# Expert results of batch 0 written from the result slots into the merge's SBUF buffer, and the second attention's preparation placed four result products earlier

## The chip, the cores and the metric

The kernel runs on one core of one Trainium2 chip. The metric is the device time of the whole program in microseconds, the median of several runs.

## The reference

Eight batches of 512 tokens with 512 features go through two layers, each a gated cross-attention and a gated feed-forward:

```python
x = x + tanh(g_xattn[0]) * L0_xattn(layernorm(x), ctx, ctx, ...)
x = x + tanh(g_ffn[0])   * L0_ffn(layernorm(x), Wc, bc, W1, b1, W2, b2)
x = x + tanh(g_xattn[1]) * L1_xattn(layernorm(x), ctx, ctx, mask, ...)
x = x + tanh(g_ffn[1])   * L1_ffn(layernorm(x), W_r, W_k, W_v, mu_r, mu_k)
```

The part at issue is `L0_ffn`, a mixture of 128 experts over groups of 32 tokens (16 groups in a batch, 128 in all). In each group each expert takes the token with its largest logit, and puts its result back on that token:

```python
perm            = (logits == max over the group's tokens)
permuted        = einsum('bntd,bntes->bnesd', grouped, perm)
inner           = relu(einsum('bnesd,esdf->bnesf', permuted, W1) + b1)
result_permuted = einsum('bnesf,esdf->bnesd', inner, W2) + b2
result          = einsum('bnesd,bntes->bntd', result_permuted, perm)
```

## The kernel before

All loops over engines are written out by hand: `build` runs five parts one behind the other on each engine (keys and values; first attention; `experts`; second attention, which is `attention` with `merge` set; `feed_forward`), and semaphores are the only order between engines. All DMAs are issued by the sync engine (SP), in program order, so that a wait on it holds back everything behind it.

**Experts.** `gather` (L2101) picks the chosen tokens with products against the choices; ACT (L2012) and DVE (L2020) bring them from PSUM into `gt`, whose last axis is the group. A set `s` has 16 groups, one batch: four tiles of 128 tokens with four groups each. `hidden` (L2119) multiplies by W1. Then come 64 result products p (L2135). Each takes the 64 groups of four batches (`h = p // 32`), and makes four experts for the two PSUM banks: partition `c * 64 + group`, 512 features. ACT (L2031) and DVE (L2056) copy the banks into a ring of RO = 4 slots that lies over `chosen` and `xc1`; a slot is one block u (p = 2u and 2u + 1), 128 partitions x 4 experts x 512, 1 MB. SP stores each slot with one DMA (L1984) to DRAM (`s_rp`), and ACT and DVE wait, before they write block u, for the store of block u - 4 (`out_st`). Blocks 0 to 15 hold batches 0 to 3, blocks 16 to 31 batches 4 to 7.

**Merge.** The second attention begins behind the products. Its steps are called at fixed numbers p from `behind` in each engine and from `load_behind` on SP. At `MERGE_AT` = 41 PE adds the experts' results to the tokens of batch 0 (`merge_tile`, L1621 and L1622 for the bias b2, L1626 for the results in `rp`: 128 experts on partitions, 4 tiles x 4 groups x 512). DVE adds that to x and normalises (L1324, L1269, L1314). At `NORM_AT` = 45 PE transposes, at `QUERIES_AT` four query products follow, at `MAXIMA_AT` the maxima of the scores, at `ROWS_AT` = 58 the transpose of the maxima, and behind the last product (p = 63) the first scores (L1606). `result_on_act` gives ACT both copies of a product while DVE is at the merge.

**Loads for it.** Behind the store of block 16 (`HALF_U`), SP waits until blocks 0 to 15 have landed (`half_written`), and loads batch 0's results with 16 DMAs (`load_experts`, L709, one for each tile and group of four, 256 KB each, 128 rows of 2 KB); the query weight (L715) follows. Behind block 22 it loads batch 1's in the same way, when PE is through with `rp`. Batches from 1 on are loaded for each turn; from batch 2 on GpSimd adds the bias (L1050).

Of the kernel before, what the change touches and what calls it, by code (L numbers as in the profile page):

```python
# [79 lines left out]
MAXIMA_AFTER = {n: (k // 2, (0, 1) if k % 2 == 0 else (2, 3)) for k, n in enumerate((49, 50, 51, 52, 53, 54, 56, 57))}  # L80
MERGE_AT, WEIGHT_AT, NORM_AT, QUERIES_AT, ROWS_AT = 41, 43, 45, (47, 49, 51, 53), 58
MAXIMA_AT = {49 + n: (n // 2, (0, 1) if n % 2 == 0 else (2, 3)) for n in range(8)}
Ahead = namedtuple("Ahead", "load_weights load_first load_keys load_second load_output_weight constants first_norm query_weights_high query_weights_low first_norm_high "
# [3 lines left out]

Behind = namedtuple("Behind", "load act dve pe")

# [464 lines left out]
def attention(nc, lay, io, early, late, sem, eight, after, front=None, turned_place=None):  # L554
# [58 lines left out]
    if route:  # L613
        allot(early, "wqh wql kl mpick kbd vals pick bc mx xr wch wcl bcol tie nstats nmv nmark nve nn mt " + small)
        allot(late, "qh ql xth xtl woh wol ath pvs atl rs rx lg gmax perm chosen pr xn x")
        allot(turned_place, "mr")
    else:
        allot(early, "wqh wql xth xtl rp xn permb b2h b2l bo x qh ql pvs woh wol pr ath atl kbd kl mpick vals pick bc b2s mx "
                     "mt rs rx sums bq " + small)
# [85 lines left out]
    def load_experts(sp, j, t):  # L705
        of = 0 if isinstance(j, int) and j < HALF else 1
        src = io["rp"][of].rearrange("u (c j a t) s d -> (u c) s j t a d", c=2, a=GT, t=NT)
        for a in range(GT):
            sp.dma_start(rp[:, t, a:a + 1], src[:, :, bass.ds(j - HALF * of, 1), t, a]).then_inc(rp_in[t], 16)  # L709
# [167 lines left out]
    def load_behind(sp, u):  # L877


        if u is None:  # L880
            sp.wait_ge(front.cleared, 1)
            load_x(sp, 0)
        if u == 7:
            load_perm(sp, 0)
            sp.dma_start(b2[:, :], io["b2"]).then_inc(w_in[2], 16)
            load_gates(sp)
            sp.dma_start(bq[:, :], io["bq"]).then_inc(c_in, 16)
        if u == HALF_U:
            front.half_written(sp)
            for t in range(NT):  # L890
                load_experts(sp, 0, t)
            load_query_weight(sp)
        if u == HALF_U + 2:
            sp.wait_ge(const, 2)
            load_keys(sp, 0)
            sp.dma_start(bo[:, :], io["bo"].partition_broadcast(P)).then_inc(bo_in, 16)
        if u == 22:
            for k, uses in TW:
                sp.wait_ge(full[k], uses.n(None, "merge", 1) + 1)
            load_perm(sp, 1)  # L900
            for t in range(NT):
                load_experts(sp, 1, t)
        if u == 24:
            load_x(sp, 1)
        if u == 28:
            load_v(sp, 0)
# [118 lines left out]
    def gpsimd(pool):  # L1025
# [17 lines left out]
        def add_experts_bias(j, ts):  # L1043

            if isinstance(j, int) and j == 2 and 0 in ts:
                pool.wait_ge(b2_in, 16)
            for t in ts:
                pool.wait_ge(rp_in[t], 16 * GT * (j + 1))
                for a in range(GT):
                    pool.tensor_tensor(rp[:, t, a], rp[:, t, a], b2s[:, :], ALU.add).then_inc(rp_biased, 1)  # L1050
# [476 lines left out]
    def tensor(pe, banks_read=None, step_of=None):  # L1527
# [82 lines left out]
        def merge_tile(i, j, t):  # L1610
# [9 lines left out]
            else:  # L1620
                pe.matmul(out[:, :], permb[:, cols], b2h[:, :], start=True, stop=False, skip_group_check=True)  # L1621
                pe.matmul(out[:, :], permb[:, cols], b2l[:, :], start=False, stop=False, skip_group_check=True)  # L1622
                pe.wait_ge(rp_in[t], 16 * GT * (j + 1))
            for a in range(GT):
# [214 lines left out]
    if merge:  # L1839
        return Engines(sync, gpsimd, scalar, vector, tensor), banks_free, ident, mhalf, \  # L1840
            Behind(load_behind, lambda act, k: scalar(act, k), lambda dve, k: vector(dve, k),
                   lambda pe, k: tensor(pe, None, k))
    ahead = Ahead(load_weights, load_first, load_first_keys, load_second, load_output_weight, constants, first_norm, query_weights_high, query_weights_low,
# [5 lines left out]
def experts(nc, sb, sem, eight, io, behind):  # L1849
# [111 lines left out]
    def sync(sp):  # L1961
# [17 lines left out]
        for u in range(EK):  # L1979
            for p in (2 * u, 2 * u + 1):  # L1980
                for q in range(2):
                    b, n = result_bank(p, q)
                    sp.wait_ge(g_free[b], n + 1)
            sp.dma_start(io["rp"][2 * u // EK][u % (EK // 2)], slot(u)).then_inc(out_st[u % RO], 16)  # L1984
            behind[0].load(sp, u)

    def half_written(sp):
        for q in range(RO):
            sp.wait_ge(out_st[q], 16 * (EK // 2 // RO))

    def written(eng, q):
        eng.wait_ge(out_st[q], 16 * (EK // RO))

    def gathered(c, s, a):

        b, _ = use(SETS * c + s, a)
        ts = slice(TS * a, TS * (a + 1))
        dst = gt[:, :, s, :, ts] if turned(c) else gt[:, s, :, :, ts]
# [23 lines left out]
    def scalar(act):  # L2022
        def results(p):
            u = p // 2
            if p % 2 == 0 and u >= RO:
                act.wait_ge(out_st[u % RO], 16 * (u // RO))
            for q in range(2):
# [19 lines left out]
    def vector(dve):  # L2047
        def results(p):
            u = p // 2
            if p % 2 == 0 and u >= RO:  # L2050
                dve.wait_ge(out_st[u % RO], 16 * (u // RO))
            for q in range(2):
# [599 lines left out]
```

## Time and profile before

| | |
|---|---|
| median of 3 runs | 1321.31 us (1316.73 to 1325.94) |
| profiled execution | 1322.05 us, span 1320.3 us |
| PE busy | 1252.8 us (95% of the span) |
| DVE, ACT, POOL busy | 887.4, 570.1, 552.6 us |
| mean granted clock of PE | 0.986 of full speed |
| DMA | 213.59 MB, mean 162 GB/s |
| chain that ended last | PE 76%, DVE 9%, DMA 5%, sync queue 3%, issue 3%, ACT 3% |

The span is that of one profiled execution. "SPq" is SP's queue of DMA issues; the duration of an issue is the time that the queue spends on it, and its landing comes later. Names like `s_rp<-e_chosen` say where a transfer goes and where it comes from; the slots appear as `e_chosen` and `e_xc`. PE is matmul, ACT is ScalarE, DVE is VectorE, POOL is GpSimd. The granted clock is a share of full speed, 2.4 GHz; a half is the lower level, 1.2 GHz.

### The profile page before, as it was taken

Reading aid. Unit: us, or ns where it says so; the run is one execution under the profiler, and the core shown is the slowest. Engines: PE = TensorE matmul, PEld = TensorE weight load, DVE = VectorE, ACT = ScalarE, POOL = GpSimd, SP = SyncE. Lnnn points to the kernel's source line nnn. Section 1 sums busy time; section 2 is a strip of 40 time slices with the busy share of each in tenths; the row PEclk is TensorE's granted clock in tenths of the full one; section 3 lists DMA queues with packets and bytes.
Section 4 is the critical chain, followed back from the end, with each engine's and each line's share of the span. In section 5 each row is a group of like instructions: output and inputs, shape, how many; then the busy total and the mean of one; then the engine's idle time right before and its main releaser. Section 6 shows DMA issues by size and latency. Waiting matters only on the chain.

```text
span 1320.3 us, 28354 instructions
## 1 busy us (share of the span) xinstructions
PE 1252.8 (95%) x10607; PEld 901.3 (68%) x10607; DVE 887.4 (67%) x1570; ACT 570.1 (43%) x1039; POOL 552.6 (42%) x456
## 2 busy tenths in 40 slices
PE   8999999999999978886999999999998999999998
PEld 7777677777777657621447666766775778887887
DVE  6985677777676455564547766766685977777762
ACT  4255245534442554453562443353336434333331
POOL 3303642553251100000339657866834644454540
PEclk9999999999999998998999999999998999999999
DMA  9885465234411678899993643563423111111100
GB/s 351 220 184 185 138 183 173 79 113 150 142 65 45 209 206 273 308 402 368 403 337 116 213 167 99 176 221 123 133 84 129 64 64 64 64 49 47 64 29 35
DMA packets 126502, 213.59 MB, mean 162 GB/s; under 512 B 27609, under 2 KB 49369, under 8 KB 122331
## 3 DMA queue, kind: packets, MB, share of 16 engines
q1 hardware_dynamic: 126427, 212.57, 48.7%
q8 instruction: 49, 0.80, 0.2%
q14 instruction: 26, 0.21, 0.1%
HBM read 129.92 MB, written 82.62 MB: 161 GB/s over the span
## 4 chain that ended last, share of the span: by engine, by line
PE 76%; DVE 9%; DMA 5%; SPq 3%; issue 3%; ACT 3%; POOL 1%; DVEq 0%; ACTq 0%; POOLq 0%
PE b L157 12%; PE b L158 11%; PE b L159 11%; PE b L1606 5%; PE b L1805 5%; PE b L1806 4%; PE b L1807 4%; PE b L1577 4%; PE b L1712 3%; PE b L1720 3%; PE b L2135 3%; PE b L2101 3%; PE b L1626 2%; PE b L2119 2%; SPq L709 2%
## 5 line engine op out<-in xcount | busy, mean ns | idle before, releaser
L1169 ACT ACTIVATE a_pr<-b 120x512 f32<-120x512 f32 x252 | 130.1, 604 | 89.3 <-PE b L1606 89.3
L1358 DVE TENSOR_REDUCE a_mx<-b 128x4 f32<-128x480 f32 x256 | 151.8, 649 | 14.6 <-PE b L1577 14.4
L1050 POOL TENSOR_TENSOR a_rp<-a_rp,a_b2s 128x512 f32<-128x512 f32 x96 | 120.4, 1291 | 26.6 <-DMA a_rp<-s_rp 26.6
L1089 POOL TENSOR_TENSOR a_atl<-a_pvs,a_ath 128x512 fp32r<-128x512 f32 x64 | 81.2, 1302 | 79.1 <-ACT a_ath L1213 79.1
L1805 PE MATMUL b<-a_woh,a_ath 128*128 128x512 f32 x256 | 104.9, 410 | 3.1 <-POOL a_atl L1089 3.1
L157 PE MATMUL b<-a_xth,a_wqh 128*128 128x512 f32 x256 | 104.2, 407 | 0.6 <-DVE a_xtl L1333 0.4
L1807 PE MATMUL b<-a_woh,a_atl 128*128 128x512 f32 x256 | 101.8, 398 | 0.0
L158 PE MATMUL b<-a_xtl,a_wqh 128*128 128x512 f32 x256 | 101.8, 398 | 0.0
L1806 PE MATMUL b<-a_wol,a_ath 128*128 128x512 f32 x256 | 101.8, 398 | 0.0
L159 PE MATMUL b<-a_xth,a_wql 128*128 128x512 f32 x256 | 101.7, 397 | 0.0
L1503 DVE SCALAR_TENSOR_TENSOR a_x<-b,a_gate,a_x 128x512 f32<-128x512 f32 (+1 forms) x64 | 47.7, 745 | 72.5 <-PE b L1807 72.5
L1034 POOL TENSOR_TENSOR a_rstd<-a_ve,a_mhalf 128x4 f32<-128x4 f32 x16 | 16.2, 1013 | 187.9 <-DVE a_ve L1280 187.9
L1577 PE MATMUL b<-a_kbd,a_qh 128*128 128x480 f32 x256 | 83.8, 388 | 4.8 <-DMA a_kbd<-s_kh 4.1
L2283 POOL TENSOR_TENSOR f_xmkl<-f_mix,f_xmkh 128x512 fp32r<-128x512 f32 x32 | 48.9, 1543 | 59.9 <-ACT f_xmkh L2295 59.9
L2325 DVE SCALAR_TENSOR_TENSOR f_mix<-f_dif,f_mu,f_xt 128x512 f32<-128x512 f32 x64 | 63.1, 1002 | 14.7 <-PE b L159 10.7
L2012 ACT ACTIVATE e_gt<-b 128x512 f32<-128x512 f32 x87 | 46.0, 598 | 48.4 <-PE b L2101 42.2
L1720 PE MATMUL b<-a_pr,a_vals 120*32 120x512 f32 x512 | 66.7, 592 | 0.0
L840 POOL TENSOR_TENSOR a_xr<-a_xr,a_mr 128x512 f32<-128x512 f32 x28 | 45.1, 1652 | 42.3 <-DMA a_mr<-s_norms 42.3
L1577 PEld LDWEIGHTS b<-a_kbd,a_qh 128*128 128x128 f32 x256 | 47.1, 188 | 23.0 <-DVE a_mx L1358 5.8
L157 PEld LDWEIGHTS b<-a_xth,a_wqh 128*128 128x128 f32 x256 | 48.4, 189 | 20.0 <-issue 7.9
L1805 PEld LDWEIGHTS b<-a_woh,a_ath 128*128 128x128 f32 x256 | 48.7, 190 | 18.6 <-issue 8.6
L2135 PE MATMUL b<-e_w,e_inner 32*64 32x512 f32 x384 | 49.8, 622 | 9.8 <-ACT e_chosen L2031 4.6
(245 smaller groups left out, 3127.3 us busy)
## 6 DMA issues: line engine op xcount, KB each, us to landing
a_rp<-s_rp SPq DMA_DIRECT2D x128, 256.0 KB, 4.6
s_x<-a_x SPq DMA_DIRECT2D x16, 1024.0 KB, 4.3
s_rp<-e_chosen SPq DMA_DIRECT2D x16, 1024.0 KB, 8.0
s_rp<-e_xc SPq DMA_DIRECT2D x16, 1024.0 KB, 8.0
e_w<-in_w SPq DMA_DIRECT2D x56, 256.0 KB, 5.1
a_xr<-in_x_t SPq DMA_DIRECT2D x8, 1024.0 KB, 6.5
a_x<-in_x SPq DMA_DIRECT2D x8, 1024.0 KB, 10.5
s_xn<-a_xn SPq DMA_DIRECT2D x8, 1024.0 KB, 4.6
```

Source lines behind the costliest of these rows:

```text
L157: pe.matmul(out, ah, bh, start=(c == 0 and not begun), stop=False)
L158: pe.matmul(out, ah, bl, start=False, stop=False)
L159: last = pe.matmul(out, al, bh, start=False, stop=(c == C - 1))
L1050: pool.tensor_tensor(rp[:, t, a], rp[:, t, a], b2s[:, :], ALU.add).then_inc(rp_biased, 1)
L1169: act.activation(pr[:, h % RING, :], bank[k][0:S2, :], ACT.Exp, scale=SCALE)\
L1358: dve.tensor_reduce(mx[:, t, :, r], bank[k][:, 0:HJ * S2].rearrange("p (a s) -> p a s", a=HJ), AX.X, ALU.max).then_inc(free[k], 1)
L1577: pe.matmul(bank[k][:, 0:HJ * S2], qh[:, r, t * P:(t + 1) * P], kbd[:, r, :], start=True, stop=True)\
L1720: ins = pe.matmul(bank["v"][a * DK:(a + 1) * DK, :], v[:, h * DK:(h + 1) * DK], pr[:, h % RING, :], start=True, stop=True)
L1805: pe.matmul(out, ath[:, m, cols], woh[:, m, :], start=(m == 0), stop=False)
L1806: pe.matmul(out, ath[:, m, cols], wol[:, m, :], start=False, stop=False)
L1807: ins = pe.matmul(out, atl[:, m, cols], woh[:, m, :], start=False, stop=(m == C - 1))
L2135: ins = pe.matmul(gbank[b][c * NH:(c + 1) * NH, :], inner[rows, k, h * NH:(h + 1) * NH], w2[k // KS][rows, k % KS, :], start=True, stop=Tr ...
```

## The change

Blocks 0 to 15 are no longer stored whole. For each half c of the partitions, the 16 groups of batch 0 (`own`) go from the slot into `rp` in SBUF, one DMA for each expert: 16 partitions x 2 KB into one partition of `rp`. The other 48 groups of the half go to DRAM with one DMA. All ten DMAs of a block count on the block's `out_st`, whose sums are now given by `stored`. The loads of batch 0's results go, and the wait for `half_written` moves from SP to PE's `merge_tile`. So that a group's place in the slot is its place in `rp`, the order of groups within a set is changed where they are gathered (`ts`) and where the other batches are loaded (`src`). `rp` is allocated first in its room. The counts of `rp_in` start at batch 1. `MERGE_AT`, `WEIGHT_AT`, `NORM_AT`, `QUERIES_AT`, `ROWS_AT` and `MAXIMA_AT` are each four lower, and batch 1's results are loaded behind block 20 rather than 22.

```diff
--- before.py
+++ after.py
@@ -78,14 +78,14 @@
 BEGUN, SCORED, EARLY_NORM = 59, 61, 57
 QUERIES_AFTER = {47: (0, 1), 49: (2,), 53: (3,)}
 MAXIMA_AFTER = {n: (k // 2, (0, 1) if k % 2 == 0 else (2, 3)) for k, n in enumerate((49, 50, 51, 52, 53, 54, 56, 57))}
-MERGE_AT, WEIGHT_AT, NORM_AT, QUERIES_AT, ROWS_AT = 41, 43, 45, (47, 49, 51, 53), 58
-MAXIMA_AT = {49 + n: (n // 2, (0, 1) if n % 2 == 0 else (2, 3)) for n in range(8)}
+MERGE_AT, WEIGHT_AT, NORM_AT, QUERIES_AT, ROWS_AT = 37, 39, 41, (43, 45, 47, 49), 54
+MAXIMA_AT = {45 + n: (n // 2, (0, 1) if n % 2 == 0 else (2, 3)) for n in range(8)}
 Ahead = namedtuple("Ahead", "load_weights load_first load_keys load_second load_output_weight constants first_norm query_weights_high query_weights_low first_norm_high "
                             "first_norm_low begin_act begin_dve begin_pe")
 
 Begun = namedtuple("Begun", "load_ahead gather emptied evict_act evict_dve on_act chosen")
 
-Behind = namedtuple("Behind", "load act dve pe")
+Behind = namedtuple("Behind", "load act dve pe rp")
 
 Front = namedtuple("Front", "cleared half_written written groups_read spare_banks banks")
 
@@ -615,7 +615,7 @@
         allot(late, "qh ql xth xtl woh wol ath pvs atl rs rx lg gmax perm chosen pr xn x")
         allot(turned_place, "mr")
     else:
-        allot(early, "wqh wql xth xtl rp xn permb b2h b2l bo x qh ql pvs woh wol pr ath atl kbd kl mpick vals pick bc b2s mx "
+        allot(early, "rp wqh wql xth xtl xn permb b2h b2l bo x qh ql pvs woh wol pr ath atl kbd kl mpick vals pick bc b2s mx "
                      "mt rs rx sums bq " + small)
     wqh, wql, woh, wol, kl, mpick, kbd, v, pick, bc, mx, ident, mhalf, gate, part, stats, mv, mark, ve, rstd, qh, ql, \
         xth, xtl, pr, ath, atl, pvs, mt, rs, rx, xn, xs = (tile[n] for n in (
@@ -704,7 +704,7 @@
 
     def load_experts(sp, j, t):
         of = 0 if isinstance(j, int) and j < HALF else 1
-        src = io["rp"][of].rearrange("u (c j a t) s d -> (u c) s j t a d", c=2, a=GT, t=NT)
+        src = io["rp"][of].rearrange("u (c j t a) s d -> (u c) s j t a d", c=2, a=GT, t=NT)
         for a in range(GT):
             sp.dma_start(rp[:, t, a:a + 1], src[:, :, bass.ds(j - HALF * of, 1), t, a]).then_inc(rp_in[t], 16)
 
@@ -886,15 +886,12 @@
             load_gates(sp)
             sp.dma_start(bq[:, :], io["bq"]).then_inc(c_in, 16)
         if u == HALF_U:
-            front.half_written(sp)
-            for t in range(NT):
-                load_experts(sp, 0, t)
             load_query_weight(sp)
         if u == HALF_U + 2:
             sp.wait_ge(const, 2)
             load_keys(sp, 0)
             sp.dma_start(bo[:, :], io["bo"].partition_broadcast(P)).then_inc(bo_in, 16)
-        if u == 22:
+        if u == 20:
             for k, uses in TW:
                 sp.wait_ge(full[k], uses.n(None, "merge", 1) + 1)
             load_perm(sp, 1)
@@ -1045,7 +1042,7 @@
             if isinstance(j, int) and j == 2 and 0 in ts:
                 pool.wait_ge(b2_in, 16)
             for t in ts:
-                pool.wait_ge(rp_in[t], 16 * GT * (j + 1))
+                pool.wait_ge(rp_in[t], 16 * GT * j)
                 for a in range(GT):
                     pool.tensor_tensor(rp[:, t, a], rp[:, t, a], b2s[:, :], ALU.add).then_inc(rp_biased, 1)
 
@@ -1620,7 +1617,10 @@
             else:
                 pe.matmul(out[:, :], permb[:, cols], b2h[:, :], start=True, stop=False, skip_group_check=True)
                 pe.matmul(out[:, :], permb[:, cols], b2l[:, :], start=False, stop=False, skip_group_check=True)
-                pe.wait_ge(rp_in[t], 16 * GT * (j + 1))
+                if i is None:
+                    front.half_written(pe)
+                else:
+                    pe.wait_ge(rp_in[t], 16 * GT * j)
             for a in range(GT):
                 col = t * P + a * G
                 last = pe.matmul(out[a * G:(a + 1) * G, :], f(permb[:, col:col + G]), rp[:, t, a, :],
@@ -1839,7 +1839,7 @@
     if merge:
         return Engines(sync, gpsimd, scalar, vector, tensor), banks_free, ident, mhalf, \
             Behind(load_behind, lambda act, k: scalar(act, k), lambda dve, k: vector(dve, k),
-                   lambda pe, k: tensor(pe, None, k))
+                   lambda pe, k: tensor(pe, None, k), rp)
     ahead = Ahead(load_weights, load_first, load_first_keys, load_second, load_output_weight, constants, first_norm, query_weights_high, query_weights_low,
                   first_norm_high, first_norm_low,
                   lambda act, n: scalar(act, n), lambda dve, n: vector(dve, n), lambda pe, n: tensor(pe, None, n))
@@ -1981,20 +1981,32 @@
                 for q in range(2):
                     b, n = result_bank(p, q)
                     sp.wait_ge(g_free[b], n + 1)
-            sp.dma_start(io["rp"][2 * u // EK][u % (EK // 2)], slot(u)).then_inc(out_st[u % RO], 16)
+            if u < EK // 2:
+                for c in range(2):
+                    at, own, e = c * NH, NG // B, 2 * EJ * u + EJ * c
+                    for j in range(EJ):
+                        sp.dma_start(behind[0].rp[e + j:e + j + 1].rearrange("s t a d -> s (t a) d"),
+                                     slot(u)[at:at + own, j, :]).then_inc(out_st[u % RO], 16)
+                    sp.dma_start(io["rp"][0][u][at + own:at + NH], slot(u)[at + own:at + NH]).then_inc(out_st[u % RO], 16)
+            else:
+                sp.dma_start(io["rp"][1][u - EK // 2], slot(u)).then_inc(out_st[u % RO], 16)
             behind[0].load(sp, u)
 
-    def half_written(sp):
+    def stored(n):
+
+        return 16 * (2 * (EJ + 1) * min(n, EK // 2 // RO) + max(n - EK // 2 // RO, 0))
+
+    def half_written(eng):
         for q in range(RO):
-            sp.wait_ge(out_st[q], 16 * (EK // 2 // RO))
+            eng.wait_ge(out_st[q], stored(EK // 2 // RO))
 
     def written(eng, q):
-        eng.wait_ge(out_st[q], 16 * (EK // RO))
+        eng.wait_ge(out_st[q], stored(EK // RO))
 
     def gathered(c, s, a):
 
         b, _ = use(SETS * c + s, a)
-        ts = slice(TS * a, TS * (a + 1))
+        ts = slice(a, GS, 4)
         dst = gt[:, :, s, :, ts] if turned(c) else gt[:, s, :, :, ts]
         return dst, gbank[b][:, :].rearrange("p (t w e) -> p w e t", t=TS, w=WG)
 
@@ -2023,7 +2035,7 @@
         def results(p):
             u = p // 2
             if p % 2 == 0 and u >= RO:
-                act.wait_ge(out_st[u % RO], 16 * (u // RO))
+                act.wait_ge(out_st[u % RO], stored(u // RO))
             for q in range(2):
                 if result_on_act(p, q):
                     b, n = result_bank(p, q)
@@ -2048,7 +2060,7 @@
         def results(p):
             u = p // 2
             if p % 2 == 0 and u >= RO:
-                dve.wait_ge(out_st[u % RO], 16 * (u // RO))
+                dve.wait_ge(out_st[u % RO], stored(u // RO))
             for q in range(2):
                 if not result_on_act(p, q):
                     b, n = result_bank(p, q)
```

## Rows read from the trace of the kernel before

**Rows 1.** Chain of waits, 540 to 720 us: start us, us, what.

```profile
596.72 8.30 DMA s_rp<-e_xc
605.11 0.62 SPq L709
...
616.57 9.74 DMA s_rp<-e_chosen
```

**Rows 2.** Windows of 10 us: stretch, length, busy us (instructions) by engine, clock, DMA share, GB/s.

```profile
590.00:600.00 10.00, 7.82 (x68) 2.02 (x64) 5.73 (x11) 5.06 (x10) 0.00 (x0) 1.00 1.01 421
...
610.00:620.00 10.00, 7.36 (x30) 1.86 (x30) 3.45 (x7) 0.00 (x0) 0.00 (x0) 0.66 1.03 343
620.00:630.00 10.00, 5.39 (x37) 1.50 (x40) 5.83 (x18) 3.67 (x8) 1.02 (x1) 0.77 1.04 384
```

**Rows 3.** Sync queue in order of time, 555 to 690 us: start, us, line, what.

```profile
558.84 2.52 SPq L1984 DMA_DIRECT2D s_rp<-e_chosen  x2
...
577.11 0.81 SPq L712 DMA_DIRECT2D a_permb<-s_perm  x1
...
580.97 0.49 SPq L887 DMA_DIRECT2D a_bq<-in_bq  x1
...
599.23 0.34 SPq L1984 DMA_DIRECT2D s_rp<-e_chosen  x1
605.11 10.66 SPq L709 DMA_DIRECT2D a_rp<-s_rp  x16
...
633.79 10.98 SPq L709 DMA_DIRECT2D a_rp<-s_rp  x16
```

**Rows 4.** PE in order of time, 575 to 700 us: start, us, line, [idle before it].

```profile
605.90 1.96 PE L2135 MATMUL b<-e_w,e_inner 32*64 32x512 f32 x16 [0.61 <-DVE e_xc L2056]
...
615.00 1.94 PE L1626 MATMUL b<-a_rp,a_permb 128*32 128x512 f32 x8 [1.65 <-DMA a_rp<-s_rp]
...
621.46 1.95 PE L2135 MATMUL b<-e_w,e_inner 32*64 32x512 f32 x16
627.56 3.69 PE L2135 MATMUL b<-e_w,e_inner 32*64 32x512 f32 x16 [4.15 <-ACT e_chosen L2031]
...
672.07 0.50 PE L1606 MATMUL b<-a_qh,a_kbd 32*120 32x512 f32 x4 [1.53 <-ACT e_xc L2031]
...
673.21 0.50 PE L1621 MATMUL b<-a_b2h,a_permb 128*128 128x512 f32 x1
...
673.87 1.07 PE L1626 MATMUL b<-a_rp,a_permb 128*32 128x512 f32 x8
674.86 0.50 PE L1621 MATMUL b<-a_b2h,a_permb 128*128 128x512 f32 x1
```

**Rows 5.** Sync queue in order of time, small transfers in five other stretches.

```profile
12.89 0.29 SPq L244 DMA_DIRECT2D kv_bv<-in_bv  x1
...
67.67 2.40 SPq L698 DMA_DIRECT2D a_kbd<-s_kh  x4
...
108.09 0.43 SPq L224 DMA_DIRECT2D s_kl<-kv_kl  x1
...
617.59 2.69 SPq L698 DMA_DIRECT2D a_kbd<-s_kh  x4
...
961.87 1.78 SPq L698 DMA_DIRECT2D a_kbd<-s_kh  x4
```

**Rows 6.** DMA issues by tensors: count, KB each, median us from issue to landing.

```profile
s_x<-a_x SPq DMA_DIRECT2D x16, 1024.0 KB, 4.3
```

**Rows 7.** Groups by line, 445 to 700 us: shapes, count, busy us, mean ns, idle before.

```profile
L2012 ACT ACTIVATE e_gt<-b 128x512 f32<-128x512 f32 x87 | 46.0, 598 | 48.4 <-PE b L2101 42.2 <-PE b L2119 6.2
...
L2020 DVE COPY e_gt<-b 128x512 f32<-128x512 f32 x41 | 27.0, 687 | 18.0 <-PE b L2101 18.0
L2031 ACT ACTIVATE e_xc<-b 128x512 f32<-128x512 f32 x41 | 23.0, 599 | 12.9 <-PE b L2135 7.6 <-DMA s_rp<-e_xc 5.1
...
L1324 DVE SCALAR_TENSOR_TENSOR a_x<-b,a_gate,a_x 128x512 f32<-128x512 f32 x8 | 6.0, 751 | 17.0 <-PE b L1626 16.9
```

## The prediction

> **What bounds the kernel now.** I read four views, all around the stage that makes and stores the 32 blocks of expert results (u = 0 to 31; each block is two result products, p = 2u and 2u+1). First the chain of waits, to see what the end hangs on there. From 596.72 us it leaves the engines: 8.3 us for a store to land, then 16 issues of L709 on the sync queue, then 9.74 us for the first store that was queued behind them [rows 1]. Second the windows. In 590 to 600 and 610 to 630 us the DMA share is 1.01 to 1.04 with 343 to 421 GB/s, while PE is busy only 5.4 to 7.8 us of every 10, and its granted clock is 0.66 of full speed between 610 and 620 us, so part of that time is spent at the lower level, 1.2 GHz, behind stretches in which PE waited [rows 2]. So this stretch is bound by stores and loads, not by PE. Third the sync queue's own timeline: block 0's store goes out at 558.84, block 16's at 599.23, that is 40.4 us for 16 blocks or 2.5 us each, and one store is one issue. Then the queue waits for the first half to land and spends 10.66 us on the 16 loads of batch 0's results (605.11 to 615.8) [rows 3]. Fourth PE's timeline: the last two products before the merge at 605.90, merge tiles that wait 1.65 us for their data at 615.00, the last product before a 4.15 us wait at 621.46 (the wait ends at 627.56), and the second attention's first scores at 672.07 [rows 4].
>
> After 672 us the program has its own pace and waits on nothing that this change moves, so I read the whole effect as a shift of that 672.07.
>
> **What is removed.** (a) The queue's wait for block 15 before it may store block 17, and the 16 loads at 0.65 us of queue time each, are gone from u = 16. What they cost PE is the 4.15 us wait at 627.56 (ACT had no free slot), and the wait of the merge for its data [rows 4]. (b) 4.2 MB (16 loads of 256 KB) are read back no more. At about 420 GB/s [rows 2] that is 10 us of transfer time, in a stretch where transfers bound.
>
> **What is added.** For each of the first 16 blocks the sync queue issues ten DMAs where it issued one: for each of two halves, four transfers of 16 partitions x 2 KB into one partition of the merge's buffer (32 KB each), and one store of the other 48 partitions. That is 144 more issues in the first half, against the 16 loads removed. The trace of before has no such transfer, so I bound the queue time of one from both sides. Back-to-back issues in order of size: four loads of keys (60 KB each) took 1.78 us at 961.87, 2.40 us at 67.67 and 2.69 us at 617.59, the last while the DMA share was full. That is 0.45 to 0.67 us each. The second store of a pair took 0.43 us; the cheapest issue I find, 4 KB, took 0.29 us, with about 0.05 us between issues [rows 5]. So the floor is 0.34 us and the ceiling 0.67. I take 0.56, the middle of the three key loads: they are the nearest rows, several small transfers one behind the other. Ten issues then take 5.6 us per block against the 2.5 us in which PE and the transfers are through with a block. The ring has four slots, so after four blocks ACT and DVE wait for slots at the queue's pace, PE waits for them, and nothing covers the difference.
>
> The Trainium skill speaks against this term: "DMA: Bandwidth & Descriptors", section "Issuing engines are not separate DMA queues", calls the sequencer's time to start a DMA usually small relative to the DMA itself. By that rule the issue term would drop out and the sum would come to the faster rival below, 1311 us. The trace disagrees already for single large stores only in part: 0.33 us of issue against 2.5 us of pace; it is the factor of ten that turns the two around [rows 3].
>
> **The sum.** Block 0's store can go out at 558.84 as before. 16 blocks x 10 x 0.56 = 90 us; the five loads of constants that sit at u = 7 keep their 4.4 us (577.11 to 581.46) [rows 3]. Block 15's last issue ends at 653. Its landing: 4.3 us, the median of a 1 MB store where the queue isn't full [rows 6]; 657.5. The merge of batch 0 now waits on PE for exactly this (it moved there from the sync queue; behind it on PE stand product 38 and all later ones, behind those ACT, DVE and the stores). It needs data at four tiles. At full clock a tile is 1.65 us (673.21 to 674.86), so 6.6 us; after a long stretch of half idle PE I expect the lower level for part of it, as a tile's eight matmuls show that took 1.94 us at 615.00 and 1.07 us at 673.87, so 10 us [rows 4]. Merge over at 667.5.
>
> From the merge's end to the scores it was 50.6 us (621.46 to 672.07). Of that the 4.15 us wait goes. Four more products now follow the merge (38 to 41; earlier they preceded it): 4 x 1.26 = 5.0 us at the store pace of 2.53 us a block. The preparation itself (norm, queries, maxima) keeps its spacing in products, so "four products sooner" moves it relative to the products and costs or saves nothing by itself. 50.6 - 4.15 + 5.0 = 51.5, so the scores come at 719.0, and the shift is +46.9 us.
>
> Terms taken at nothing: the second batch's loads, now issued at u = 20, take the queue 11 us as before (633.79, 10.98 us) [rows 3]; they lie beside the queries' products on PE, and three free slots cover them; without the slots ACT would wait as it does today. The query weight's load at u = 16 lies beside the merge. The 10 us of transfers saved buys nothing once issues bound. The evictions of gathered tokens write every fourth element where they wrote four in a row. Nearest rows: the same eviction, which reads PSUM scattered, takes 598 ns on ACT, and one that reads and writes in a row 599 ns [rows 7], so scattering cost nothing on the reading side. I take 0, which is also the lower end, since the same elements are moved; the upper end is the surcharge of a two-input step against a plain copy on DVE, 751 less 687 ns [rows 7], for 41 evictions under 3 us.
>
> The profiled execution took 1322.05 us (span 1320.3), 0.7 us above the median of the three runs, 1321.31, so the two bases agree. 1322 + 46.9 gives **1369 us**. With 0.45 us an issue: 17.6 us less, 1351. With 0.67: 17.6 more, 1387.
>
> **Rivals.**
> *The single target partition binds (1439 us in full).* In a 128-partition store the 16 DMA engines share about 420 GB/s [rows 2], 26 GB/s each. If all 16 engines write to one place and that place takes no more than one engine's rate, a 32 KB transfer takes 1.25 us, eight of them 10 us per block, and 16 blocks 160 us in place of 90: +117 us, 1439. If transfers to the two halves overlap, it is 5 us per block, and the issue term binds again. For it: every write of a transfer goes to one partition, and no transfer in the trace does that. Against it: no row shows such a limit, and engines that drift apart overlap several targets. It decides from 0.7 us per small transfer.
> That one place exists is a rule of the Trainium skill: "SBUF — State Buffer", section "Door 1: The DMA port swizzle", gives eight partitions one port of 27.2 GB/s, with 27.6 GB/s measured on partitions 0 to 3. No run here shows it yet; its figure would make a block 9.6 us.
>
> *Faster (1311 us): the issues are hidden.* If a small DMA costs the queue under 0.25 us, blocks keep 2.5 us, the merge starts four products (5 us) sooner on data that is there, runs in 6.6 us, and the 51.5 us follow: the merge begins near 603 and is over at 610, scores at 661, -11 us. For it speaks the full DMA share of today, which is what the change relieves. Against it: the cheapest issue I find takes 0.29 us, and the break-even (160 issues that take no more than 43 us) is at 0.27 us each.
>
> *No change (about 1333 us at the floor).* With 0.34 us an issue the first half takes 54 us, the shift is +11 us, under 1%.
>
> **Chances.** Issue-bound forecast 0.48; the target partition binds wholly or in part 0.32; hidden, faster by over 1% 0.05, within 1% 0.08 (1% is what a measurement of this kernel can tell from no change); slower than 1% by the floor price or by slot waits of another kind, 0.07. So slower 0.87, same 0.08, faster 0.05. The range runs from 1340, just below the forecast at 0.45 us less a few us for the merge at full clock, to 1436, which takes in nearly all of the partition's rival; the likeliest case's own range is 1345 to 1390.
>
> **What would show it.** Right: the first 16 blocks' stores spread over 80 to 100 us with the sync queue issuing nearly without a gap, gaps between issues of 0.45 to 0.67 us, DMA share well under 1 there, ACT and DVE waiting for slots, PE's granted clock below full in that stretch. The partition's rival: DMA share full while GB/s is far below 400, issues of over 1 us because the queue is backed up, landings of 20 us and more. Faster: L709's first burst gone and the pace still 2.5 us per block. In all cases the 4.15 us wait behind the merge should be gone and the stretch from the merge's end to the scores be near 51.5 us; if that stretch grows by more than 5 us, my reading that the preparation's place is neutral is wrong.

## The result: 8.1% slower, and the profile after

The changed kernel took 1432.71 us (median of 4 runs, 1430.65 to 1433.79), against 1323.62 us for the kernel before on the same chips: ratio 1.0813, 95% interval 1.0781 to 1.0844. The profiled execution has a span of 1431.5 us, 111.2 us above that of before.

The page's chain by engine and by line, in which the sync queue's share has gone from 3% to 10%:

```profile
PE 72%; SPq 10%; DVE 8%; ACT 5%; issue 3%; DMA 2%; POOL 0%; ACTq 0%; DVEq 0%; POOLq 0%
PE b L157 12%; PE b L158 11%; PE b L159 11%; SPq L1988 8%; PE b L1603 5%; PE b L1805 4%; PE b L1806 4%; PE b L1807 4%; PE b L1574 4%; PE b L1712 4%; PE b L1720 3%; ACT e_gt L2024 3%; PE b L1626 2%; PE b L2113 2%; SPq L1990 1%
```

Sync queue, in order of time (start, us, line). L1988 issues the small transfers, L1990 the stores of 48 partitions, L1992 whole stores. They answer to [rows 3]:

```profile
577.35 2.55 SPq L1988 DMA_DIRECT2D a_rp<-e_chosen  x4
579.94 0.58 SPq L1990 DMA_DIRECT2D s_rp<-e_chosen  x1
...
720.67 0.58 SPq L1990 DMA_DIRECT2D s_rp<-e_xc  x1
721.41 0.37 SPq L1992 DMA_DIRECT2D s_rp<-e_chosen  x1
```

Block 0 leaves at 577.35, not at 558.84, and block 15's last issue ends at 721.25: 143.9 us for 16 blocks, where it was 40.4 for the same blocks.

Windows (PE, PEld, DVE, ACT, POOL busy, granted clock, DMA share, GB/s), against [rows 2]:

```profile
600.00:610.00 10.00, 4.87 (x24) 1.16 (x22) 1.29 (x2) 1.08 (x2) 0.00 (x0) 0.50 0.60 126
...
640.00:650.00 10.00, 3.69 (x16) 0.87 (x16) 1.29 (x2) 1.09 (x2) 0.00 (x0) 0.50 0.51 104
...
660.00:670.00 10.00, 3.69 (x16) 0.88 (x16) 1.29 (x2) 1.08 (x2) 0.00 (x0) 0.50 0.65 138
```

In these windows PE is busy under half of the time. The DMA share is 0.51 to 0.65, where it was 1.01 to 1.04. The granted clock is 0.50, which is 1.2 GHz, in stretches in which PE stood waiting. Neither PE nor the transfers bind here.

PE, against [rows 4]: first merge product on batch 0's results, last one, next expert product, first scores:

```profile
725.36 1.94 PE L1626 MATMUL b<-a_rp,a_permb 128*32 128x512 f32 x8 [12.99 <-DMA s_rp<-e_xc]
...
732.70 1.07 PE L1626 MATMUL b<-a_rp,a_permb 128*32 128x512 f32 x8
733.69 1.95 PE L2147 MATMUL b<-e_xc,e_inner 32*64 32x512 f32 x16
...
784.25 0.50 PE L1603 MATMUL b<-a_qh,a_kbd 32*120 32x512 f32 x4 [1.52 <-ACT e_xc L2043]
```

The stretch from the merge's end (733.69) to the scores (784.25) is 50.6 us, the same as before. Everything was lost ahead of it.

Groups of the evictions, from 445 to 600 us, against [rows 7] (598 and 687 ns there):

```profile
L2024 ACT ACTIVATE e_gt<-b 128x512 f32<-128x512 f32 x87 | 84.6, 1131 | 28.0 <-PE b L2113 21.3 <-PE b L2131 6.6
L2032 DVE COPY e_gt<-b 128x512 f32<-128x512 f32 x41 | 42.2, 1082 | 23.0 <-PE b L2113 22.8
```

### The profile page after: what moved, and what is told of

Its sections match the earlier page's. It is cut to its first block, busy times and chain, and to the rows that moved or that the text cites. A ratio compares the mean times of both kernels' runs of the same rounds, so it can differ in the third digit from the quotient of the medians.

```text
span 1431.5 us, 28488 instructions
## 1 busy us (share of the span) xinstructions
PE 1283.9 (90%) x10607; PEld 914.8 (64%) x10607; DVE 899.1 (63%) x1570; ACT 607.7 (42%) x1039; POOL 554.5 (39%) x456
## 4 chain that ended last, share of the span: by engine, by line
PE 72%; SPq 10%; DVE 8%; ACT 5%; issue 3%; DMA 2%; POOL 0%; ACTq 0%; DVEq 0%; POOLq 0%
PE b L157 12%; PE b L158 11%; PE b L159 11%; SPq L1988 8%; PE b L1603 5%; PE b L1805 4%; PE b L1806 4%; PE b L1807 4%; PE b L1574 4%; PE b L1712 4%; PE b L1720 3%; ACT e_gt L2024 3%; PE b L1626 2%; PE b L2113 2%; SPq L1990 1%
## 5 line engine op out<-in xcount | busy, mean ns | idle before, releaser
L2147 PE MATMUL b<-e_w,e_inner 32*64 32x512 f32 x384 | 64.9, 792 | 59.8 <-DVE e_chosen L2068 29.9
L2024 ACT ACTIVATE e_gt<-b 128x512 f32<-128x512 f32 x87 | 84.6, 1131 | 28.0 <-PE b L2113 21.3
L2147 PEld LDWEIGHTS b<-e_w,e_inner 32*64 32x64 f32 x384 | 15.5, 163 | 100.9 <-issue 50.0
```

The lines of the kernel that those rows point to most:

```text
L2024: act.activation(dst, src, ACT.Copy).then_inc(g_free[b], 1)
```

## The experiments

Times are medians, and a ratio is to the kernel before, measured together with the variant. Where only one run was made there is no ratio. "The pace" is the time from one block of results to the next on the queue, 8.5 us in the change where no issue is out of the ordinary.

### e1: evictions in order again

```diff
-        ts = slice(a, GS, 4)
+        ts = slice(TS * a, TS * (a + 1))
...
+                own = rp[:, a, t, :] if i is None else rp[:, t, a, :]
```

> The change with the evictions of gathered tokens writing four elements in a row again; batch 0's rows then lie in another order in the merge's buffer, and the merge reads them there. Nothing else differs. Theory A (the scattered write is what made an eviction take 1131 ns on ACT and 1082 ns on DVE, and is worth the whole 18.5 us by which block 0's store came later): evictions back at 598 and 687 ns, block 0's store near 559 us, the run 16 to 20 us under the change, 1413 to 1417 us. Rival (the 18.5 us are mostly transfers of weights that came later, the evictions are covered): under 8 us gained. Issues of small transfers unchanged in both, 9.0 us a block.

Measured: 1419.69 us, ratio 1.0704 (1.0649 to 1.0759). The evictions are back at 598 and 687 ns, block 0's first transfer goes out at 562.34 us, 15.0 us sooner than in the change, and the run is 13 us shorter. The blocks' pace stayed. So the first theory has the cause right; its size, 16 to 20 us, was too large.

### e2: the ten transfers of a block, all to DRAM, in the kernel before

```diff
-            sp.dma_start(io["rp"][2 * u // EK][u % (EK // 2)], slot(u)).then_inc(out_st[u % RO], 16)
...
+                    for j in range(EJ):
+                        sp.dma_start(io["rp"][0][u][at:at + own, j], slot(u)[at:at + own, j, :]).then_inc(out_st[u % RO], 16)
+                    sp.dma_start(io["rp"][0][u][at + own:at + NH], slot(u)[at + own:at + NH]).then_inc(out_st[u % RO], 16)
```

> The kernel before, with the store of each of the first 16 blocks cut into the same ten transfers (eight of 16 partitions x 2 KB, two of 48 partitions), all to DRAM; batch 0 is loaded as before. Issue theory (a small transfer costs the sync queue 0.8 us or more wherever it goes): 9 us a block, 144 us for 16 blocks, 1321 + 100 = about 1420 us. Target theory (it is the one partition written that backs the queue up): issues at 0.45 to 0.6 us, 4.5 to 6 us a block, so + 32 to + 56 us, 1353 to 1377 us.

Measured: 1406.2 us, ratio 1.0604 (1.0535 to 1.0673). That is 81 us of loss without one byte going from a slot straight into the merge's buffer, with loads and schedule as before. The pace is 7.5 us a block, between the two expectations and nearer to the issue theory. The chain of waits runs along the queue (start us, us, what). Here is half a block, from one store to the next (L1988 issues the small transfers, L1989 the stores):

```profile
654.60 0.42 SPq L1989
...
655.18 0.31 SPq L1988
...
655.53 1.86 SPq L1988
...
657.43 0.42 SPq L1988
...
657.90 0.42 SPq L1988
...
658.36 0.42 SPq L1989
```

Small issues take 0.30 to 0.43 us here and 0.50 to 0.59 in the change. One issue in five takes 1.86 us here; in the change one in five takes about 1.7 to 1.8.

### e3: half of each row

```diff
-...rearrange("s t a d -> s (t a) d"), slot(u)[at:at + own, j, :])
+...rearrange("s t a d -> s (t a) d")[:, :, 0:D // 2], slot(u)[at:at + own, j, 0:D // 2])
...
```

> The change with half of each row in the small transfers (16 x 1 KB in place of 16 x 2 KB), and batch 0's merge over those 256 columns only; the other half of batch 0's expert results is left out. As many issues, descriptors and targets. Issue or descriptor theory: still 9.0 us a block, 1430 us. Target theory (bytes into one place): a small transfer goes from 0.88 to about 0.5 us, 5 to 5.5 us a block, 16 blocks 56 to 64 us less, 1368 to 1376 us.

Measured: 1426.34 us (one run). With half the bytes in the small transfers the median issue is the same to the nanosecond (590 ns). Only the landing is faster, 2.9 against 4.3 us. So the bytes of the small transfers aren't the bound.

### e4: sixteen partitions as target

```diff
-                        sp.dma_start(behind[0].rp[e + j:e + j + 1].rearrange("s t a d -> s (t a) d"),
+                        n = u // 8 * 8 + c * EJ + j
+                        sp.dma_start(behind[0].rp[16 * (u % 8):16 * (u % 8) + own, n // GT, n % GT],
```

> The change with each small transfer written into 16 partitions of the same buffer, one row each, in place of 16 rows of one partition (batch 0's results then lie in wrong places). As many issues, descriptors and bytes, from the same sources. Issue theory: 9.0 us a block, 1430 us. Target theory: 4.5 to 6 us a block, 48 to 72 us less, 1360 to 1384 us.

Measured: 1426.98 us (one run). The line of the small transfers, with issue durations min/median/max in ns, first in the change, then here:

```profile
L1988 SPq DMA_DIRECT2D a_rp<-e_chosen x64: 502/590/1802, 577.3 to 701.6; - x64
L1988 SPq DMA_DIRECT2D a_rp<-e_xc x64: 502/590/2714, 594.7 to 720.0; - x64
DMA to landing us min/median/max: 3.4/4.3/5.9
```

```profile
L1989 SPq DMA_DIRECT2D a_rp<-e_chosen x64: 507/590/2074, 572.4 to 694.4; - x64
L1989 SPq DMA_DIRECT2D a_rp<-e_xc x64: 507/590/1798, 589.8 to 712.3; - x64
DMA to landing us min/median/max: 1.9/2.7/3.5
```

The single partition costs 1.6 us of landing and nothing of the pace. So the partition's rival falls as the bound of the change.

### e5: one whole store in place of two of 48 partitions

```diff
-                    sp.dma_start(io["rp"][0][u][at + own:at + NH], slot(u)[at + own:at + NH]).then_inc(out_st[u % RO], 16)
+                sp.dma_start(io["rp"][0][u], slot(u)).then_inc(out_st[u % RO], 16)
```

> The change with nine issues a block in place of ten: the eight small transfers one behind the other and then one store of the whole slot (batch 0's rows are stored too, which nobody reads). In the change every issue takes 0.50 to 0.59 us but one in five takes 1.7 us. Count theory (the queue stalls on every fifth issue, whatever it is): the long issue moves through the block, 9 x 0.63 + 9/5 x 1.15 = 7.7 us a block, 20 us less than the change, about 1412 us. Store theory (a long issue stands two behind each large store, because the large store takes the generator of descriptors long): exactly one long issue a block, always the second small transfer behind the store, 9 x 0.63 + 1.2 to 3.2 = 6.9 to 8.9 us a block, 1400 to 1431 us; the place of the long issue tells.

Measured: 1405.73 us (one run), 27 us less for one issue of ten, and with more bytes. First the chain of waits in the change, half a block from one store to the next:

```profile
616.07 0.58 SPq L1990
...
616.69 0.50 SPq L1988
...
617.23 1.78 SPq L1988
...
619.06 0.59 SPq L1988
...
619.69 0.59 SPq L1988
...
620.32 0.58 SPq L1990
```

Then here, a whole block of nine issues from store to store:

```profile
652.41 0.58 SPq L1990
...
653.15 0.51 SPq L1988
...
653.70 1.37 SPq L1988
...
655.11 0.59 SPq L1988
...
655.74 0.59 SPq L1988
...
656.37 0.59 SPq L1988
...
657.01 0.59 SPq L1988
...
657.64 0.59 SPq L1988
...
658.27 0.59 SPq L1988
...
658.90 0.58 SPq L1990
```

In both, the long issue is the second behind the store. With one store a block, all 14 blocks whose first small transfer comes directly behind a slot's store have it at that place; block 0 comes behind loads of weights and block 8 behind the five constants, and in block 8 every small issue takes 0.51 to 0.59 us. Some blocks have a further long issue elsewhere. So the long issue sits there by order and not by count, and the count theory falls. The pace is 6.5 us in the block shown and 6.9 us on average, without the constants. The place speaks for the store theory; that the generator of descriptors is the reason isn't shown by it. The store of 1 MB has the shorter long issue, 1.37 us against 1.78 behind 384 KB, so a time that grows with the size of the store doesn't fit either.

### e6, e7: the other two parts alone, in the kernel before

```diff
-MERGE_AT, WEIGHT_AT, NORM_AT, QUERIES_AT, ROWS_AT = 41, 43, 45, (47, 49, 51, 53), 58
+MERGE_AT, WEIGHT_AT, NORM_AT, QUERIES_AT, ROWS_AT = 37, 39, 41, (43, 45, 47, 49), 54
```

> The kernel before with the preparation four products sooner (merge at product 37, the others with it) and batch 1's loads behind block 20; the stores and the loads of batch 0 as before. Theory (the place of the preparation is neutral by itself, the merge waits for batch 0's loads wherever it stands): the loads go out at 605 us as before, the merge waits until 611 us on PE, the ring's slots are then free for the products behind it, so -4 to +4 us. Rival (the earlier merge makes PE idle before the loads have landed and nothing is won behind it): + 5 to + 12 us.

Measured: 1325.24 us, ratio 1.0008 (0.9992 to 1.0025, ten runs). Neutral, as the first theory has it: the merge waits 8.23 us for its first load in place of 2.47, and the wait of 4.15 us behind it is gone.

```diff
...
-        ts = slice(TS * a, TS * (a + 1))
+        ts = slice(a, GS, 4)
```

> The kernel before with the evictions of gathered tokens writing every fourth element, and the loads of the results in the matching order. Theory: evictions 1131 and 1082 ns, block 0's store 13 to 19 us later and the run as much slower, + 13 to + 19 us. Rival (what comes behind is bound by transfers and takes part of it back, since weights and other loads have landed by then): + 5 to + 12 us.

Measured: 1339.78 us, ratio 1.0133 (1.0107 to 1.0159), which is 15 us slower. The evictions take 1131 and 1081 ns. Added to the kernel before it costs 15 us, and taken out of the change it gives back 13 (e1).

### e8: loads spread, and e10: merge later

```diff
...
+        if u in SPREAD:
+            if u == min(SPREAD):
+                front.half_written(sp)
+            for t in SPREAD[u]:
+                load_experts(sp, 0, t)
...
+    SPREAD = {18: (0, 1), 19: (2,), 20: (3,)}
```

> An attempt at the aim of the change by another way: the kernel before, with batch 0's 16 loads not in one burst behind block 16 but behind blocks 18 (two tiles), 19 and 20 (one each), and the wait for the first half at block 18, where it has landed. Merge at 41 as before. Theory (the 4.15 us wait of PE behind the merge comes from the burst that holds block 17's store back): that wait goes, the merge waits 1 to 3 us for its last tile, -2 to -6 us. Rival (this stretch is bound by the bytes, in whatever order): within 2 us of the kernel before.

Measured: 1338.54 us, ratio 1.0112 (1.0073 to 1.0151), 14 us slower, so both expectations fail. The loads now queue behind the stores of blocks 17 and 18, and PE waits in the merge itself, 12.03 and 4.07 us:

```profile
622.38 1.93 PE L1629 MATMUL b<-a_rp,a_permb 128*32 128x512 f32 x8 [12.03 <-DMA a_rp<-s_rp]
...
633.18 1.94 PE L1629 MATMUL b<-a_rp,a_permb 128*32 128x512 f32 x8 [4.07 <-DMA a_rp<-s_rp]
```

e10 moves the numbers of e6 by two the other way (`MERGE_AT` 43, the others with it, batch 1's loads behind block 23).

> The kernel before with the preparation two products later (merge at product 43, the others with it, batch 1's loads behind block 23). Theory (the place of the preparation is neutral in both directions while transfers bound this stretch, as the move by four to the other side was): within 3 us of the kernel before. Rival (the merge now finds its data landed and PE no longer waits 1 to 3 us a tile, at full clock): -3 to -8 us, a version that beats both.

Measured: 1332.07 us, ratio 1.0055 (1.0037 to 1.0073). It is 8 us slower, so both expectations fail. For its loads the merge waits 2.44 us at most, but before its third tile it waits for DVE (PE, start us, us, line, [idle before it]):

```profile
632.60 0.80 PE L1621 MATMUL b<-a_b2h,a_permb 128*128 128x512 f32 x1 [11.54 <-DVE a_x L1324]
```

DVE stood 18.40 us before an eviction of a result product, for a slot whose store had been issued at 621.30 us behind the 16 loads, and came to the merge's sums only after it. So the place of the preparation is neutral four products sooner (e6) and not two later.

### e9: the stores in rows of 2 KB

```diff
-                    sp.dma_start(io["rp"][0][u][at + own:at + NH], slot(u)[at + own:at + NH]).then_inc(out_st[u % RO], 16)
+                    to = io["rp"][0][u][at + own:at + NH].rearrange("p s d -> (p s) d").rearrange("(s p) d -> p s d", s=EJ)
+                    sp.dma_start(to, slot(u)[at + own:at + NH]).then_inc(out_st[u % RO], 16)
```

> The change with the two stores of 48 partitions a block written to DRAM in rows of 2 KB in place of 8 KB (the rows of the other batches then lie in other places). As many issues and bytes. Row theory (in the change the second issue behind each store waits about 1.15 us, because a store of 8 KB rows occupies the generator of descriptors): with rows of 2 KB that wait changes; if it goes, 2.3 us a block and some 35 us in all, about 1397 us. Rival (the wait has nothing to do with the rows' length, it comes with any store of hundreds of KB): block pace still 8.7 us, 1430 us.

Measured: 1434.41 us (one run). The long issues are at the same places and take mostly 1.74 to 1.94 us, so the length of the rows isn't the reason.

### e11 and e12: both repairs, and two queues

e11 has the edits of e1 and e5 together.

> The change with both repairs that have been measured one by one: evictions in order again (-13 us alone) and one store of the whole slot in place of the two of 48 partitions (-27 us alone, nine issues a block). If the two are independent, the sum: 1433 - 13 - 27 = 1393 us, block pace 6.5 us against 2.5 us in the kernel before, so still 69 us above it. Rival (with the issues as the bound an earlier start of block 0's store is worth less, or more): more than 5 us off that sum.

Measured: 1388.78 us, ratio 1.0503 (1.046 to 1.0546). That is 44 us less than the change, where the sum of the parts is 40, so the two costs are independent to within the 5 us of the expectation.

e12 stands on e11; the cut shows what is added to it.

```diff
-                for c in range(2):
+                for c in range(1):
...
+            if p % 2 and u < EK // 2:
...
+                for j in range(EJ):
+                    act.dma_start(behind[0].rp[e:e + 1].rearrange("s t a d -> s (t a) d"),
+                                  slot(u)[NH:NH + NG // B, j, :]).then_inc(out_st[u % RO], 16)
```

> The variant with both repairs (in order, one store a block: 1389 us, 6.5 us a block), with the four small transfers of the second half issued from ACT's queue in place of the sync queue's, once all four bank copies of the block are done. The sync queue then has five issues a block, ACT four beside its copies. Queue theory (each engine's queue spends its own time on an issue, and the sync queue's time is the bound): 5 x 0.63 + 0.8 = about 4 us a block, 16 x 2.5 = 40 us less, about 1349 us, still above the kernel before. Rival (both queues share what generates the descriptors, and that is the bound): 6.5 us a block still, 1385 to 1395 us.

Measured: 1356.12 us, ratio 1.0215 (1.0176 to 1.0254). That is 33 us less than e11 with the same transfers, only issued by two engines: the sync queue's own time was the bound. Block 0 and block 15 on that queue:

```profile
567.73 3.65 SPq L1989 DMA_DIRECT2D a_rp<-e_chosen  x4
571.42 0.58 SPq L1991 DMA_DIRECT2D s_rp<-e_chosen  x1
...
644.01 3.14 SPq L1989 DMA_DIRECT2D a_rp<-e_xc  x4
647.19 0.58 SPq L1991 DMA_DIRECT2D s_rp<-e_xc  x1
```

644.01 less 567.73 over 15 blocks is 5.1 us, where e11 has 7.1 counted in the same way, constants included. The expectation was about 4. What stands in the way is first ACT, whose evictions and issues now take turns (ACTq is ACT's queue of DMA issues; start us, us, line):

```profile
600.99 1.09 ACT L2044 ACTIVATE e_xc<-b 128x512 f32<-128x512 f32 x2 [3.55 <-issue]
602.24 4.14 ACTq L2053 DMA_DIRECT2D a_rp<-e_xc  x4
606.48 1.09 ACT L2044 ACTIVATE e_chosen<-b 128x512 f32<-128x512 f32 x2 [4.40 <-issue]
607.73 3.21 ACTq L2053 DMA_DIRECT2D a_rp<-e_chosen  x4
611.04 1.08 ACT L2044 ACTIVATE e_chosen<-b 128x512 f32<-128x512 f32 x2 [3.48 <-issue]
```

From one block's evictions to the next it is 5.49 and 4.56 us, all of it ACT's issues, ACT's evictions and short gaps. In the chain of waits from 590 to 610 us ACT's issues are 71% and its evictions 22%, and no transfer is in it. From 570 to 647 us ACT's issues are 47%, the sync queue's 12%, and waits for a store to land 16%. (The traced execution, 1362.73 us, is the slowest of the four.) So part of the time is transfers, and the windows show them near their limit (columns as above):

```profile
600.00:610.00 10.00, 5.59 (x32) 1.39 (x32) 2.08 (x3) 2.17 (x4) 0.00 (x0) 0.64 0.90 264
610.00:620.00 10.00, 6.85 (x36) 1.48 (x32) 3.46 (x5) 2.89 (x6) 0.00 (x0) 0.67 1.08 156
620.00:630.00 10.00, 5.54 (x32) 1.26 (x32) 1.29 (x2) 2.17 (x5) 0.00 (x0) 0.84 1.04 297
```

The DMA share is 0.90 to 1.08 at 156 to 297 GB/s, where whole stores made it full at 421 [rows 2]. That fits the single target partition, but no run of this variant with other targets was made, so it isn't shown. Neither version beats the kernel before.

## Why the prediction was right or wrong

Right were the direction and the mechanism: the sync queue's time for ten issues a block sets the pace of the first half. e2 and e12 show the queue; e3 and e4 show that neither the bytes of the small transfers nor their target set the pace. Right too: the wait behind the merge went, the landing came 4.1 us after the last issue's end (forecast 4.3), the merge took 8.3 us (10), and from there to the scores it was 50.6 us (51.5). The preparation's place is neutral for this move (e6), though not for every one (e10).

Wrong: the size, 46.9 us forecast against 109. Two steps failed.

**"I take 0.56."** 16 blocks and the constants were to take 94.4 us and took 143.9, which is 49.5 us more. I had taken one price for all ten issues from bursts of four loads of 60 KB [rows 5]. It is not even the middle of the three, as I called it: that is 0.60 (2.40 us for four), and 0.56 lies halfway between the ends. With 0.60 the forecast would have been 1375 us, so that slip is the small part. A half block of the change, from 616.07 to 620.32 (above), is 4.25 us: five issues at 0.50 to 0.59 and a gap of 0.04, 3.1 us, and 1.15 us more for the issue that comes second behind the store. Twice that is 8.5 us a block. Of the 2.9 us above my 5.6, 2.3 are those two long issues, 0.6 the plain price of 0.62 with its gap. Over the 16 blocks there are 30 long issues outside the constants, 34.5 us, and 9.6 us of plain price. The long issue was missing from the bounds altogether: my ceiling of 0.67 an issue gave 1387 us. The rows did not give it: the burst at 617.59 does stand behind two whole stores, and issue by issue it is 0.50, 0.71, 0.62 and 0.74 us. A chain of stores and small transfers that keeps the queue busy without a pause stood nowhere in the trace of before, and a ceiling taken from rows of another context was no ceiling. The rest, some 5 us over the 16 blocks, are mostly single issues that are longer still, up to 2.7 us.

**"I take 0, which is also the lower end"**, with an upper end of "under 3 us", on the evictions that write every fourth element. Between the two profiles it was 18.5 us at block 0's first issue (558.84 to 577.35). Some of that is the difference of one profile from another: with the evictions of before, block 0 leaves at 560.56 to 563.24 in e1, e2, e6, e8 and e10. By the medians it is 13 us (e1) and 15 us (e7). I argued from a row on scattered reads of PSUM to scattered writes into SBUF, which is another thing, and gave the bound from a surcharge that had nothing to do with it. Before, every four elements lay in 16 bytes in a row; after, they lay 16 bytes apart. ACT went from 598 to 1131 ns and DVE from 687 to 1082. The Trainium skill has the rule, in "SBUF — State Buffer", section "Door 1: The DMA port swizzle": SBUF has lines of 16 bytes, and each access that crosses to a new one pays. The traces agree in direction, at 1.9 times on ACT and 1.6 on DVE. I had read that section for its ports and not for this.

The two terms and the rest add up at the scores: 18.5 + 49.5 - 0.2 for landing, - 1.7 for the merge, - 0.9 behind it = 65.2 above the forecast 719.0, and they came at 784.25.

**The rival that hit the number.** The partition's rival said 1439 us, and 1433 was measured, but its mechanism isn't the one at work: with sixteen target partitions or half the bytes the pace stays. Two of its own signs were absent, landings of 20 us (4.3) and a full DMA share (0.50 to 0.65 in the windows from 590 to 720 us). The third, issues of over 1 us, was there, one in five; but e2 has them too, 1.86 us each, with DRAM as the target. A time near a rival's is no proof of it. My range of 1340 to 1436 holds the measured time only because I had stretched it for this rival; that is luck, and the likeliest case's own range, 1345 to 1390, missed it by 43 us. What the prediction took from the Trainium skill on the ports ("SBUF — State Buffer", section "Door 1: The DMA port swizzle") isn't refuted: the landing is 1.6 us longer with one partition. That simply isn't the bound while the queue's issues are.

**Faster and no change.** They needed an issue of at most 0.27 and 0.34 us, and the median is 0.59. By the same working the 4.2 MB that aren't read back bought nothing, since the transfers had stopped being the bound; no run tests that alone.

Open: why the second issue behind a large store waits. It isn't the rows' length (e9), nor the count of issues (e5), and stores of 384 KB and 1 MB both do it (1.15 and 0.8 us more), while the burst at 617.59 before, behind whole stores too, shows none. Open too is what a plain issue's time consists of. The small ones take 0.59 us when they go from SBUF to SBUF and 0.42 when they go to DRAM. But the stores take part in that although they go to DRAM in both: 0.58 us behind small SBUF-to-SBUF transfers and 0.42 behind small ones to DRAM (e2); and a whole slot's store takes 0.33 us at the median in the kernel before and 0.58 in e5. So the time that a row shows for an issue also depends on what was issued ahead of it.

## What to carry to other kernels

Price a DMA in three currencies, bytes, landing, and the issuing queue's time, and when one transfer is cut into ten, sum the third over a period of the pipeline and compare it with the period. If issues move to an engine that also computes, sum that engine's issues and its instructions, as e12's ACT shows. Price an issue in its context: behind what it will stand counts as much as what it is. And a layout that is moved so that one transfer becomes contiguous makes another access scattered; look that one up with its own row or measure it, a row on the other side (reads for writes, PSUM for SBUF) doesn't bound it.

## What the runs showed of the hardware

- In an unbroken row of issues of one queue, the second issue behind a store of 384 KB takes mostly 1.7 to 1.9 us in place of 0.4 to 0.6, whether it goes to SBUF (the change, e9) or to DRAM (e2). Behind a store of 1 MB it takes mostly 1.4 us (e5). The one directly behind takes mostly 0.30 to 0.51.
- A plain issue of 16 rows takes the queue 0.42 us in a row that goes to DRAM (e2) and 0.59 us in a row from SBUF to SBUF, the same with 16 or 32 KB (e3) and with 1 or 16 target partitions (e4). A store to DRAM in such a row takes 0.42 or 0.58 us in the same way.
- ACT's queue takes about the same for such an issue, 0.61 and 0.63 us at the median (e12), and ACT's evictions stand between its issues.
- 32 KB into one partition land in 4.3 us (the change), into 16 partitions in 2.7 us (e4), and 16 KB into one in 2.9 us (e3).
- A 128x512 copy from PSUM whose elements land 16 bytes apart takes 1131 ns on ACT and 1082 on DVE, against 598 and 687 with four in a row (the change and e7 against before and e1).
